# Output projection and router with fp32 operands in place of three fp16 products

## The chip, the cores and the metric

The kernel runs on one core of one Trainium2 chip. The metric is the device time of one launch in microseconds (us). Engines are named as in the profile: PE is TensorE (PEld its weight loads), DVE is VectorE, ACT is ScalarE, POOL is GpSimd, and SP issues most of the DMA transfers.

## What is computed

A block of a gated cross-attention model on 64 batches of 128 tokens with 256 features, all fp32: normalise, cross-attend to a context, add; normalise again, choose one of 32 experts by a router, run that expert's two-layer network, add.

```python
# x: (64, 128, 256), ctx: (64, 128, 192), 16 heads of 16, 32 experts of hidden size 64
x = x + tanh(g_xattn) * xattn(layernorm(x), ctx)
#   xattn: q = h @ wq + bq; k = y @ wk + bk; v = y @ wv + bv
#          out = softmax(q k^T / 4) v, heads side by side
#          return out @ wo + bo                      <- the output projection
x = x + tanh(g_ffn) * ffn(layernorm(x))
#   ffn: logits = h @ router_w.T + router_b          <- the router
#        e = argmax(logits)
#        return relu(relu(h @ w1[e] + b1[e]) @ w2[e] + b2[e])
```

## The kernel before

The program has two parts. The first goes over 16 groups of four batches (512 tokens). The second goes over 96 tiles of 128 tokens that a scatter has sorted by expert.

**The group loop.** Every engine runs the same software pipeline, and the engines are tied by semaphores only. In one step, `step(s)`, the group `s` is in its attention and output projection; `a` (two groups ahead) gets its normalised input transposed and its q, k and v; `n1` (one ahead) has its score maxima taken; `f` (one behind) is in its second normalisation and router; `r` (two behind) is ranked and scattered. The tensor engine's step has two phases. First come 16 chunks, each with scores (L1068), transposed scores (L1084) and the product with v (L1101, whose operands are fp32), between which ACT takes exponentials and DVE takes maxima. Then comes the tail, in this order: k and q of `a`, the transposes of the attention's output (L1199), v of `a`, the transposes of the normalised output (L1216), the transposes of the router's input (L1223), the output projection, and the router. q and k go through two DRAM images to be stacked by head (`q_image`, `k_image`, then `qstk`, `kstk`), and the next step's first scores wait for the last of these transfers. In the last two steps (groups 14 and 15) there is no group `a`, and so no k, q, v and no transfer of q in the tail.

**Three fp16 products.** q, k, the output projection, the router and the experts' products split each fp32 operand into a high fp16 part and a low fp16 rest, and multiply high by high, low by high and high by low into one PSUM bank. The pairs are in `THREE`, and all of these products are issued by `split_matmul` (L1148). For the output projection ACT copies the transposed output S[t] to fp16 (L721), DVE subtracts that copy from S[t] to get the low part (L846, called from L933), and PE waits for `at_lo` before its 24 products of 256 columns a group. For the router ACT copies AV[t] (L732), DVE subtracts (L846, from L936), and PE waits for `x2t_lo` before its 24 products of 32 columns. DVE then reads the projection (L945, `x2_done`) and the logits (L853, `lg_done`). The weights' two parts are made once, at the start (L638, L651 on ACT; L788, L800 on DVE).

`at` lies in the buffer `xt`, and `x2t` in the upper half of each row of `ot`. SP's queue is in order: after the stacks it issues the row of maxima (L418, waits for `m_done`) and the next residual input (L423, waits for `x2_done`).

Of the kernel before, what the change touches and what calls it, by code (L numbers as in the profile page):

```python
# [32 lines left out]
P = 128  # L33
# [7 lines left out]
KT = D // P  # L41
# [55 lines left out]
def build(nc, x, ctx_t, g2, wq, bq, wk, bk, wv, bv, wo, bo, rw, rb, w1, b1, w2, b2, out):  # L97
    es = ExitStack()
    with es:
# [26 lines left out]
        wq_s = sb("wq_s", [P, 2, KT, D], F16)  # L126
        wk_s = sb("wk_s", [P, 2, 2, D], F16)
        wv_s = sb("wv_s", [P, 2, 2, D], F16)
        wo_s = sb("wo_s", [P, 2, KT, D], F16)
        rw_s = sb("rw_s", [P, 2, KT, E], F16)  # L130
        rb_b = sb("rb_b", [P, E])
        bqk = sb("bqk", [P, 2, KT])
        bqk8 = sb("bqk8", [P, 2, KT])
# [35 lines left out]
        rec = sb("rec", [P, GB, HEADS])  # L169

        an = ot[:, :, 0:D]
        at = xt
        x2 = sb("x2", [P, 2, GB, ROW])
        st2 = sb("st2", [P, GB, 6])
        mv2 = sb("mv2", [P, GB, 2])
# [8 lines left out]
        bo_b = ot_flat[:, 2 * P:2 * P + D]  # L184
        b2raw = ot_flat[0:E, 4 * P:4 * P + D]
        rw_raw = ot_flat[:, 6 * P:6 * P + KT * E].rearrange("p (k e) -> p k e", k=KT)
        x2t = ot[:, :, D:2 * D].bitcast(F16)
        lg = sb("lg", [P, GB, E])
        lmax = sb("lmax", [P, GB])
        pick = sb("pick", [P, GB, E])  # L190
# [51 lines left out]
        ln1_st ln1_mv ln1_sm xn_done y_hi y_t xt_ready xt_hi xt_lo q_ready q_hi q_lo k_ready k_hi k_lo  # L242
        v_ready v_done
        s_ready s_max mt_ready m_done st_ready exp_done av_ready av_out o_ready nrm_r nrm_done at_ready
        at_hi at_lo xb_done y_ready x2_done ln2_st ln2_mv ln2_sm xn2_done x2t_ready x2t_hi x2t_lo
        lg_ready lg_done route hot_done rk_ready rk_read rk_link pos_done ids_done
        ew_r8 ew_hi ew_lo
        t_link p_rows t_cols t_tr t_rows
# [366 lines left out]
        def _(act):  # L615
# [16 lines left out]
            act.wait_ge(s_["bias_in"], 16 * 8)  # L632
            a_.activation(bqk8[:], bqk[:], ACT.Copy, scale=WS).then_inc(s_["w_hi"], 1)
            a_.activation(b2raw[:], b2raw[:], ACT.Copy, scale=WS).then_inc(s_["w_hi"], 1)
            a_.activation(rw_raw[:], rw_raw[:], ACT.Copy, scale=WS).then_inc(s_["w_hi"], 1)
            act.wait_ge(s_["w_hi"], 5)
            a_.copy(b2hl[:, 0, :], b2raw[:]).then_inc(s_["b2_hi"], 1)
            a_.copy(rw_s[:, 0, :, :], rw_raw[:]).then_inc(s_["b2_hi"], 1)  # L638
            a_.copy(bvb[:], bvc[:].unsqueeze(2).to_broadcast([P, KT, P])).then_inc(s_["bv_wide"], 1)
            act.wait_ge(s_["w_in2"], 32)  # L640
            scaled(wraw2[:, 0:2, :])
# [4 lines left out]
            act.wait_ge(s_["tanh_done"], 1)  # L646
            a_.activation(wraw2[:, 2:4, :], wraw2[:, 2:4, :], ACT.Copy, scale=WS).then_inc(s_["w_raw8"], 1)
            act.wait_ge(s_["w_raw8"], 7)
            a_.activation(wraw2[:, 2:4, :], wraw2[:, 2:4, :], ACT.Identity, scale=tg[:, 0:1]).then_inc(s_["w_raw8"], 1)
            act.wait_ge(s_["w_raw8"], 8)  # L650
            a_.copy(wo_s[:, 0, :, :], wraw2[:, 2:4, :]).then_inc(s_["w_hi"], 1)  # L651

            def exp_chunk(g, c):
                act.wait_ge(s_["st_ready"], g.count(CHUNKS, c + 1))
# [33 lines left out]
            def step(s):  # L688
                a, n1, g, f = s.plus(2), s.plus(1), s, s.plus(-1)
                for c in range(CHUNKS):  # L690
                    if g.real():
                        exp_chunk(g, c)
                        if c % 4 == 2 and c > 4:
                            attn_out(g, c // 4 - 1)
                    if n1.real() and c in MAX_ROW:
                        max_row(n1, MAX_ROW[c])
                if a.real():
                    for t in range(KT):
                        act.wait_ge(s_["xt_ready"], a.count(2, t + 1))
                        wait(act, s_["y_ready"], a.count(2, -4))  # L700
                        a_.copy(xt[:, 0, t, :], M[t][:]).then_inc(s_["xt_hi"], 1)
                if g.real():
                    attn_out(g, 3)
                for t in range(KT):
                    if a.real():
                        act.wait_ge(s_["k_ready"], a.count(2, t + 1))
                        wait(act, k_out, a.count(64))
                        a_.activation(ks[:, 0, t, :], ST[t][:], ACT.Identity, bias=bqk8[:, 1, t:t + 1]).then_inc(s_["k_hi"], 1)
                    if n1.real() and t == 0:
                        max_row(n1, 3)  # L710
                if a.real():
                    for t in range(KT):
                        act.wait_ge(s_["q_ready"], a.count(2, t + 1))
                        wait(act, q_out, a.count(64))
                        a_.activation(qs[:, 0, t, :], M[t][:], ACT.Identity, bias=bqk8[:, 0, t:t + 1]).then_inc(s_["q_hi"], 1)  # L715
                if g.real():
                    for t in range(KT):
                        act.wait_ge(s_["at_ready"], g.count(2, t + 1))
                        if a.real():
                            act.wait_ge(s_["q_ready"], a.count(2, 2))  # L720
                        a_.copy(at[:, 0, t, :], S[t][:]).then_inc(s_["at_hi"], 1)  # L721
                if a.real():
                    for t in range(2):
                        act.wait_ge(s_["v_ready"], a.count(2, t + 1))
                        wait(act, s_["av_ready"], a.count(CHUNKS, -CHUNKS))
                        vv = v[:, a.par, t * 1024:t * 1024 + 1024].rearrange("p (h d) -> p h d", d=32)[:, :, 0:DH]
                        a_.activation(vv, ST[t][:].rearrange("p (h d) -> p h d", d=DH), ACT.Copy,
                                      scale=1.0 / WS).then_inc(s_["v_done"], 1)
                if f.real():
                    for t in range(KT):  # L730
                        act.wait_ge(s_["x2t_ready"], f.count(2, t + 1))
                        a_.copy(x2t[:, t, :], AV[t][:]).then_inc(s_["x2t_hi"], 1)  # L732
                if a.real():

                    expert_raw(a)
                    expert_hi(a)
# [38 lines left out]
        def _(dve):  # L775
# [7 lines left out]
            dve.wait_ge(s_["w_hi"], 2)  # L783
            v_.tensor_tensor(wq_s[:, 1, :, :], wraw[:, 0:2, :], wq_s[:, 0, :, :], ALU.subtract).then_inc(s_["w_lo"], 1)
            v_.tensor_tensor(wk_s[:, 1, :, :], wraw[:, 2:4, :], wk_s[:, 0, :, :], ALU.subtract).then_inc(s_["w_lo"], 1)
            dve.wait_ge(s_["b2_hi"], 2)
            v_.tensor_tensor(b2hl[:, 1, :], b2raw[:], b2hl[:, 0, :], ALU.subtract).then_inc(s_["b2_lo"], 1)
            v_.tensor_tensor(rw_s[:, 1, :, :], rw_raw[:], rw_s[:, 0, :, :], ALU.subtract).then_inc(s_["w_lo"], 1)  # L788

            v_.memset(kstk[:, :, 0, :, :], 0.0).then_inc(s_["dve_set"], 1)  # L790
            dve.wait_ge(s_["w_hi"], 6)
# [4 lines left out]
            dve.wait_ge(s_["gb_a"], 1)  # L796
            dve.wait_ge(s_["tanh_done"], 1)
            v_.tensor_scalar(gbias[:], gbias[:], tg[:, 0:1], None, ALU.mult).then_inc(s_["gb_done"], 1)
            dve.wait_ge(s_["w_hi"], 7)
            v_.tensor_tensor(wo_s[:, 1, :, :], wraw2[:, 2:4, :], wo_s[:, 0, :, :], ALU.subtract).then_inc(s_["w_lo"], 1)  # L800
            dve.wait_ge(s_["pool_set"], 1)

            def x_stats(b):
# [78 lines left out]
            def step(s):  # L882
# [46 lines left out]
                if nxt.real():  # L929
                    stats_2(st1, mv1, "ln1_st", "ln1_mv", nxt, 0)  # L930
                if g.real():
                    for t in range(KT):
                        lo_part(at[:, 1, t, :], S[t][:], at[:, 0, t, :], "at_hi", g.count(2, t + 1), "at_lo")  # L933
                if f.real():
                    for t in range(KT):
                        lo_part(x2t[:, KT + t, :], AV[t][:], x2t[:, t, :], "x2t_hi", f.count(2, t + 1), "x2t_lo")  # L936
                if g.real():
                    dve.wait_ge(s_["xb_done"], g.count(1, 1))

                    pg = g.plus(-2)  # L940
                    if pg.real():
                        wait(dve, scat[pg.par], pg.halved(16 * GB, 16 * GB))
                    for t in range(2):
                        dve.wait_ge(s_["y_ready"], g.count(2, t + 1))
                        v_.scalar_tensor_tensor(out=x2[:, g.par, 2 * t:2 * t + 2, 0:D],  # L945
                                                in0=M[t][:].rearrange("p (b n) -> p b n", b=2), scalar=1.0 / WS,
                                                in1=xres[:, 2 * t:2 * t + 2, :], op0=ALU.mult, op1=ALU.add
                                                ).then_inc(s_["x2_done"], 1)
# [96 lines left out]
        def _(pe):  # L1045
# [5 lines left out]
                last = t_.matmul(AV[0][:, 0:D], bvb[:, t, :], wraw2[:, 2 + t, :], start=(t == 0), stop=(t == KT - 1))  # L1051
            last.then_inc(s_["bvwo_ready"], 1)
            pe.wait_ge(s_["pool_set"], 1)
            pe.wait_ge(s_["w_lo"], 5)

            def scores(n1, c):

                b, cc = c // 4, c % 4
                if c == 0:
                    pe.wait_ge(stk[n1.par], n1.halved(128, 128))  # L1060
                    wait(pe, s_["at_lo"], n1.count(2, -2))
                if c == 1:
                    wait(pe, s_["lg_done"], n1.count(1, -2))
                if c >= 2:
# [24 lines left out]
            def times_v(g, c):  # L1089
# [3 lines left out]
                if cc == 0:  # L1093
                    if b >= 2:
                        pe.wait_ge(s_["av_out"], g.count(4, b - 1))
                    else:
                        wait(pe, s_["x2t_lo"], g.count(2, -4 + b + 1))
                        wait(pe, s_["nrm_done"], g.count(4))
                for i in range(CH):
                    h = (b * HEADS + CH * cc + i) * 32  # L1100
# [52 lines left out]
            def step(s):  # L1153
# [70 lines left out]
                        last.then_inc(s_["x2t_ready"], 1)  # L1224
                if g.real():

                    pe.wait_ge(s_["at_lo"], g.count(2, 2))
                    if a.real():
                        pe.wait_ge(s_["q_lo"], a.count(2, 2))
                    elif n1.real():  # L1230
# [3 lines left out]
                    for b in range(GB):  # L1234
                        tok = slice(b * P, (b + 1) * P)
                        last = split_matmul(M[b // 2][:, (b % 2) * D:(b % 2) * D + D],
                                            [(at[:, i, t, tok], wo_s[:, j, t, :]) for t in range(KT) for i, j in THREE])
                        if b % 2:
                            last.then_inc(s_["y_ready"], 1)
                if f.real():  # L1240

                    pe.wait_ge(s_["x2t_lo"], f.count(2, 2))
                    for b in range(GB):
                        tok = slice(b * P, (b + 1) * P)
                        last = split_matmul(S[0][:, b * E:(b + 1) * E],
                                            [(x2t[:, i * KT + t, tok], rw_s[:, j, t, :]) for t in range(KT) for i, j in THREE])
                    last.then_inc(s_["lg_ready"], 1)

            schedule(pe, step)
# [95 lines left out]
```

## Time and profile before

| what | value |
|---|---|
| median of 3 runs | 1111.49 us (1101.32 to 1111.63) |
| span of the profiled execution | 1114.1 us |
| PE busy | 790.7 us (71%), 7430 instructions |
| PE weight loads busy | 531.1 us (48%) |
| DVE busy | 589.2 us (53%), 1575 instructions |
| ACT busy | 481.1 us (43%) |
| POOL busy | 481.3 us (43%) |
| mean granted clock of PE | 0.738 of full speed |

The profile is one execution; shares are of its span. Matmuls are pipelined, so a busy PE isn't PE at its peak. [...]

### The profile page before, as it was taken

To read this page: it belongs to the slowest core of one execution; us is meant where nothing else is said; L and a number is where in the kernel's file an instruction comes from. 1 tells how busy PE (TensorE), PEld (TensorE's weight loads), DVE (VectorE), ACT (ScalarE), POOL (GpSimd) and SP (SyncE) were. 2 spreads that over 40 slices of the span, in tenths; PEclk is the share of its full clock that TensorE was granted. 3 is DMA by queue.
4 is the path that set the end of the run, shared out by engine and by line. 5 is a ranking of instruction groups with operands and counts; after the bars stand their busy time and mean duration, and the time that the engine had idled before them with its cause. 6 is when DMAs were issued, how large, how long until landed. Compare 5 with 4: busy or idle time off the path is not lost.

```text
span 1114.1 us, 24048 instructions
## 1 busy us (share of the span) xinstructions
PE 790.7 (71%) x7430; PEld 531.1 (48%) x7431; DVE 589.2 (53%) x1575; ACT 481.1 (43%) x1045; POOL 481.3 (43%) x703
## 2 busy tenths in 40 slices
PE   0458696968677696969678686868775048878783
PEld 0235465645455465646445555646454035545451
DVE  3253455546455455545544565644534238677783
ACT  3223353435244343435343453524351037667673
POOL 9321324361626344352625344261333506555564
PEclk9765867669586867667695987958696558687886
DMA  3753627264553627173553527344210334343340
GB/s 90 175 106 85 114 64 156 63 125 87 100 112 95 115 74 160 49 143 79 108 106 100 115 85 154 82 67 102 53 31 29 134 94 131 107 126 109 109 114 19
DMA packets 76676, 110.55 MB, mean 99 GB/s; under 512 B 11542, under 2 KB 62875, under 8 KB 73504
## 3 DMA queue, kind: packets, MB, share of 16 engines
q1 hardware_dynamic: 68320, 90.61, 37.2%
q0 software_dynamic: 8256, 18.53, 4.7%
q8 instruction: 71, 1.16, 0.5%
q14 instruction: 29, 0.24, 0.1%
HBM read 70.68 MB, written 42.27 MB: 101 GB/s over the span
## 4 chain that ended last, share of the span: by engine, by line
PE 43%; DMA 21%; issue 15%; POOL 11%; DVE 3%; SPq 2%; ACT 2%; another core or an unknown queue 1%; POOLq 1%; ACTq 0%; DVEq 0%
DMA qstk<-q_image 14%; PE AV L1101 11%; PE S L1068 10%; PE ST L1084 8%; DMA q_image<-qs 7%; POOL out L604 6%; PE M L1148 4%; PE ST L1148 4%; PE M L1125 2%; POOL carry_p L471 1%; SPq L405 1%; POOL expert_rows L595 1%; DVE qs L848 1%; ACT qs L715 1%; PE M L1116 1%
## 5 line engine op out<-in xcount | busy, mean ns | idle before, releaser
L817 DVE TENSOR_REDUCE mx<-S 128x4 f32<-128x512 f32 x256 | 174.9, 689 | 304.0 <-PE S L1068 283.0
L657 ACT ACTIVATE pt<-ST 128x512 f32<-128x512 f32 x256 | 152.4, 596 | 349.9 <-PE ST L1084 336.8
L1068 PE MATMUL S<-kstk,qstk 96*128 96x128 f16 x1024 | 144.8, 290 | 155.6 <-DMA qstk<-q_image 141.6
L1068 PEld LDWEIGHTS S<-kstk,qstk 96*128 96x128 f16 x1024 | 90.5, 126 | 216.3 <-DMA qstk<-q_image 107.2
L1101 PE MATMUL AV<-pt,v 128*32 128x128 f32 x2048 | 147.0, 373 | 22.8 <-ACT pt L657 18.6
L528 POOL TENSOR_TENSOR w1s<-w1r,w1s 128x512 f32 (+1 forms) x16 | 18.4, 1150 | 328.5 <-ACT w2s L686 328.5
L1084 PE MATMUL ST<-qstk,kstk 98*128 98x128 f16 x1024 | 142.9, 285 | 0.1
L1084 PEld LDWEIGHTS ST<-qstk,kstk 98*128 98x128 f16 x1024 | 101.9, 134 | 4.4 <-issue 2.8
L1148 PE MATMUL ST<-qs,w1s 128*128 128x128 f16 x576 | 71.0, 259 | 20.9 <-ACT yin L755 9.9
L1101 PEld LDWEIGHTS AV<-pt,v 128*32 128x32 f32 x2048 | 48.0, 129 | 68.9 <-issue 37.7
L1267 PE MATMUL S<-ident,yin 128*128 128x128 f32 x192 | 47.8, 339 | 44.7 <-DVE yin L1012 32.1
L747 ACT CAST qs<-S 128x256 f16<-128x256 f32 x96 | 35.6, 371 | 91.6 <-PE S L1267 85.6
L587 POOL DMA_INDIRECT expert_rows<-x,posi x64 | 63.3, 990 | 17.2 <-issue 16.9
L1148 PEld LDWEIGHTS ST<-qs,w1s 128*128 x576 | 48.9, 112 | 45.0 <-issue 36.9
L471 POOL TENSOR_TENSOR carry_p<-zero_e 128x1 f32<-128x1 f32 x97 | 23.0, 237 | 105.3 <-DVE posn L1033 69.7
L1012 DVE TENSOR_SCALAR yin<-x 128x256 f32<-128x256 f32 x96 | 39.6, 412 | 33.8 <-DMA x<-expert_rows 33.2
L604 POOL DMA_INDIRECT out<-xin,posn x48 | 48.2, 1005 | 18.0 <-issue 18.0
L604 POOL DMA_INDIRECT out<-xn,posn x48 | 47.9, 999 | 17.9 <-issue 17.9
L1148 PE MATMUL M<-wo_s,xt 128*128 128x256 f16 x384 | 46.0, 278 | 11.2 <-DVE xt L846 11.2
L1267 PEld LDWEIGHTS S<-ident,yin 128*128 128x128 f32 x192 | 28.1, 173 | 53.4 <-DVE yin L1012 32.9
L565 POOL TENSOR_TENSOR ids<-ids,group_c 128x4 int32<-128x4 int32 x16 | 3.2, 198 | 113.0 <-DVE mv L810 113.0
L1018 DVE TENSOR_TENSOR qs<-S,qs 128x256 f16<-128x256 f32 x96 | 40.1, 418 | 15.5 <-ACT qs L747 15.1
(190 smaller groups left out, 1606.1 us busy)
## 6 DMA issues: line engine op xcount, KB each, us to landing
x<-expert_rows SPq DMA_DIRECT2D x96, 130.0 KB
xin<-x SPq DMA_DIRECT2D x16, 512.0 KB, 4.2
yin<-ctx_t SPq DMA_DIRECT2D x16, 512.0 KB, 5.2
k_image<-ks SPq DMA_DIRECT2D x64, 128.0 KB
q_image<-qs SPq DMA_DIRECT2D x64, 128.0 KB
kstk<-k_image SPq DMA_DIRECT2D x32, 256.0 KB, 6.7
qstk<-q_image SPq DMA_DIRECT2D x32, 256.0 KB, 8.9
xres<-x SPq DMA_DIRECT2D x16, 512.0 KB, 9.4
```

Source lines behind the costliest of these rows:

```text
L587: g_.indirect_dma_start(out=rows[:, :], out_offset=bass.IndirectOffsetOnAxis(ap=posi[:, b:b + 1], axis=0), in_=x2[:, r.par, b, :], in_offs ...
L604: g_.indirect_dma_start(out=out, out_offset=bass.IndirectOffsetOnAxis(ap=ido[:, m:m + 1], axis=0), in_=yo[m], in_offset=None, bounds_check ...
L657: a_.activation(pt[:, c % NPT, :], ST[c % 2][:], ACT.Exp, scale=0.25 / (WS * WS)).then_inc(s_["exp_done"], 1)
L747: a_.copy(gx[:, n % 2, 0, :, :], S[n % 2][:, 0:D].rearrange("p (k t) -> p k t", k=KT)).then_inc(s_["f_hi"], 1)
L817: v_.reduce_max(mx[:, b, CH * cc:CH * cc + CH], S[(c + 1) % 2][:].rearrange("p (h t) -> p h t", h=CH), X).then_inc(s_["s_max"], 1)
L1012: v_.tensor_scalar(gn[:, n % 2, :], gt[:, n, 0:D], gt[:, n, D:D + 1], gt[:, n, D + 1:D + 2], ALU.mult, ALU.add).then_inc(s_["f_norm"], 1)
L1018: v_.tensor_tensor(gx[:, n % 2, 1, :, :], S[n % 2][:, 0:D].rearrange("p (k t) -> p k t", k=KT), gx[:, n % 2, 0, :, :], ALU.subtract).then_ ...
L1068: last = t_.matmul(S[(c + 1) % 2][:, i * P:(i + 1) * P], qstk[0:STACK, n1.par, hp, b * P:(b + 1) * P], kstk[0:STACK, n1.par, cc // 2, hp, ...
L1084: last = t_.matmul(ST[c % 2][:, i * P:(i + 1) * P], kstk[0:STACK + 2, g.par, cc // 2, hp, b * P:(b + 1) * P], qstk[0:STACK + 2, g.par, hp, ...
L1101: last = t_.matmul(AV[b % 2][32 * i:32 * i + 32, cc * P:(cc + 1) * P], v[:, g.par, h:h + 32], pt[:, c % NPT, i * P:(i + 1) * P], start=Tru ...
L1148: last = t_.matmul(bank, w, m, start=(n == 0), stop=(n == len(pairs) - 1))
L1267: last = t_.transpose(S[n % 2][:, k * P:(k + 1) * P], gn[:, n % 2, k * P:(k + 1) * P], ident[:])
```

## The change

The weights `wo_s` and `rw_s` and the operands `at` and `x2t` are kept in fp32, in the same bytes as the two fp16 parts before. ACT's copies write fp32, DVE's four subtractions a group are gone with their semaphores, and each product is one `matmul` of fp32 operands, so eight a group in place of 24 for the projection and eight in place of 24 for the router. All waits on the low parts become waits on ACT's copies (`at_done`, `x2t_done`). The order of the work on each engine is otherwise the same.

```diff
-        wo_s = sb("wo_s", [P, 2, KT, D], F16)
-        rw_s = sb("rw_s", [P, 2, KT, E], F16)
+        wo_s = sb("wo_s", [P, KT, D])
+        rw_s = sb("rw_s", [P, KT, E])
-        at = xt
+        at = xt[:].rearrange("p a k t -> p (a k t)").bitcast(F32).rearrange("p (k t) -> p k t", k=KT)
-        x2t = ot[:, :, D:2 * D].bitcast(F16)
+        x2t = ot[:, :, D:2 * D]
...
-            a_.activation(wraw2[:, 2:4, :], wraw2[:, 2:4, :], ACT.Identity, scale=tg[:, 0:1]).then_inc(s_["w_raw8"], 1)
-            act.wait_ge(s_["w_raw8"], 8)
-            a_.copy(wo_s[:, 0, :, :], wraw2[:, 2:4, :]).then_inc(s_["w_hi"], 1)
+            a_.activation(wo_s[:], wraw2[:, 2:4, :], ACT.Identity, scale=tg[:, 0:1]).then_inc(s_["w_hi"], 1)
...
-                        a_.copy(at[:, 0, t, :], S[t][:]).then_inc(s_["at_hi"], 1)
+                        a_.copy(at[:, t, :], S[t][:]).then_inc(s_["at_done"], 1)
...
-                        a_.copy(x2t[:, t, :], AV[t][:]).then_inc(s_["x2t_hi"], 1)
+                        a_.copy(x2t[:, 2 * t:2 * t + 2, :], AV[t][:].rearrange("p (u n) -> p u n", u=2)).then_inc(s_["x2t_done"], 1)
...
-                    for t in range(KT):
-                        lo_part(at[:, 1, t, :], S[t][:], at[:, 0, t, :], "at_hi", g.count(2, t + 1), "at_lo")
-                if f.real():
-                    for t in range(KT):
-                        lo_part(x2t[:, KT + t, :], AV[t][:], x2t[:, t, :], "x2t_hi", f.count(2, t + 1), "x2t_lo")
-                if g.real():
...
-                    pe.wait_ge(s_["at_lo"], g.count(2, 2))
+                    pe.wait_ge(s_["at_done"], g.count(2, 2))
...
-                                            [(at[:, i, t, tok], wo_s[:, j, t, :]) for t in range(KT) for i, j in THREE])
+                                            [(at[:, t, tok], wo_s[:, t, :]) for t in range(KT)])
...
-                    pe.wait_ge(s_["x2t_lo"], f.count(2, 2))
+                    pe.wait_ge(s_["x2t_done"], f.count(2, 2))
...
-                                            [(x2t[:, i * KT + t, tok], rw_s[:, j, t, :]) for t in range(KT) for i, j in THREE])
+                                            [(x2t[:, 2 * t + b // 2, (b % 2) * P:(b % 2) * P + P], rw_s[:, t, :]) for t in range(KT)])
```

## Rows read from the trace of the kernel before

**Rows 1.** The page: chain of work that ended last, shares of the span by line.

```profile
DMA qstk<-q_image 14%; PE AV L1101 11%; PE S L1068 10%; PE ST L1084 8%; DMA q_image<-qs 7%; POOL out L604 6%; PE M L1148 4%; PE ST L1148 4%; PE M L1125 2%; POOL carry_p L471 1%; SPq L405 1%; POOL expert_rows L595 1%; DVE qs L848 1%; ACT qs L715 1%; PE M L1116 1%
```

**Rows 2.** The waits of all engines: who waited for whom; us in total, times, longest.

```profile
PE S L1068 <- DMA qstk<-q_image: 141.6, 15, 15.8
```

**Rows 3.** The chain that ended last, one step's tail: start, length, what.

```profile
518.72 2.60 PE M L1148 x12
523.28 4.83 DMA q_image<-qs
529.41 9.74 DMA qstk<-q_image
```

**Rows 4.** Timeline, same tail: start, length, engine, line [idle before it <- releaser].

```profile
525.72 1.07 ACT L721 CAST xt<-S 128x512 f16<-128x512 f32 x2 [3.68 <-PE S L1216]
525.95 1.04 PE L1223 MATMUL AV<-ident,xn 128*128 128x128 f32 x8
526.33 1.29 DVE L846 TENSOR_TENSOR xt<-S,xt 128x512 f16<-128x512 f32 x2 [1.37 <-ACT xt L721]
527.68 2.79 PE L1148 MATMUL M<-wo_s,xt 128*128 128x256 f16 x24 [0.69 <-DVE xt L846]
530.31 0.75 PE L1148 MATMUL S<-rw_s,ot 128*128 128x32 f16 x24
530.51 0.69 DVE L945 SCALAR_TENSOR_TENSOR x<-M,xres 128x512 f32<-128x512 f32 x1 [0.33 <-PE M L1148]
531.63 0.41 SPq L423 DMA_DIRECT2D xres<-x  x1
```

**Rows 5.** Groups by form, whole span: shapes xcount | busy us, mean ns | idle before.

```profile
L1051 PE MATMUL AV<-xres,ot 128*128 128x256 f32 x4 | 2.1, 671 | 12.9 <-ACT ot L639 12.9
L1051 PEld LDWEIGHTS AV<-xres,ot 128*128 128x128 f32 x4 | 1.2, 323 | 12.7 <-ACT ot L639 12.6
L664 ACT COPY ot<-AV 128x512 f32<-128x512 f32 x64 | 37.2, 581 | 2.6 <-PE AV L1101 2.6
```

**Rows 6.** Timeline at the start of the span, PE and PEld.

```profile
12.89 2.07 PE L1051 MATMUL AV<-xres,ot 128*128 128x256 f32 x4 [12.89 <-ACT ot L639]
28.29 1.94 PE L1125 MATMUL M<-ident,xn 128*128 128x128 f32 x8 [13.33 <-POOL xn L558]
30.45 0.15 PEld L1148 LDWEIGHTS ST<-ys,wk_s 128*128 128x128 f16 x1 [0.28 <-issue]
```

**Rows 7.** Window: stretch, length, PE, PEld, DVE, ACT, POOL busy, granted clock, DMA, GB/s.

```profile
12.90:15.00 2.10, 2.06 (x4) 1.16 (x4) 1.30 (x3) 1.18 (x4) 2.04 (x5) 1.00 0.00 0
```

**Rows 8.** The chain after the last transfer of q: start, length, what.

```profile
816.39 1.30 DVE xt L846 x2
...
821.12 0.25 PE ST L1084 x4
...
844.95 3.86 PE M L1148 x24
...
849.52 0.20 DVE lg L853
...
859.68 0.70 DVE ot L846
860.43 1.65 PE S L1148 x24
```

**Rows 9.** Windows of one wait, two chunk loops and group 15's projection.

```profile
629.00:631.00 2.00, 1.78 (x35) 1.57 (x33) 1.67 (x4) 1.43 (x3) 0.22 (x1) 1.00 1.02 176
635.00:637.00 2.00, 0.00 (x0) 0.00 (x0) 0.00 (x0) 0.00 (x0) 1.78 (x3) 0.67 1.08 142
637.90:662.50 24.60, 21.28 (x276) 14.15 (x277) 15.25 (x37) 11.89 (x24) 14.60 (x26) 0.77 0.25 87
733.90:762.20 28.30, 27.76 (x276) 17.97 (x277) 15.40 (x37) 12.17 (x24) 12.66 (x21) 0.50 0.12 41
844.00:849.00 5.00, 5.00 (x44) 4.02 (x43) 2.83 (x5) 1.17 (x2) 0.00 (x0) 0.67 0.00 0
```

More of the change, by code:

```diff
@@ L244, in build @@
         s_ready s_max mt_ready m_done st_ready exp_done av_ready av_out o_ready nrm_r nrm_done at_ready
-        at_hi at_lo xb_done y_ready x2_done ln2_st ln2_mv ln2_sm xn2_done x2t_ready x2t_hi x2t_lo
+        at_done xb_done y_ready x2_done ln2_st ln2_mv ln2_sm xn2_done x2t_ready x2t_done
         lg_ready lg_done route hot_done rk_ready rk_read rk_link pos_done ids_done
@@ L634, in _ @@
             a_.activation(b2raw[:], b2raw[:], ACT.Copy, scale=WS).then_inc(s_["w_hi"], 1)
-            a_.activation(rw_raw[:], rw_raw[:], ACT.Copy, scale=WS).then_inc(s_["w_hi"], 1)
+            a_.activation(rw_s[:], rw_raw[:], ACT.Copy, scale=WS).then_inc(s_["w_hi"], 1)
             act.wait_ge(s_["w_hi"], 5)
             a_.copy(b2hl[:, 0, :], b2raw[:]).then_inc(s_["b2_hi"], 1)
-            a_.copy(rw_s[:, 0, :, :], rw_raw[:]).then_inc(s_["b2_hi"], 1)
             a_.copy(bvb[:], bvc[:].unsqueeze(2).to_broadcast([P, KT, P])).then_inc(s_["bv_wide"], 1)
@@ L785, in _ @@
             v_.tensor_tensor(wk_s[:, 1, :, :], wraw[:, 2:4, :], wk_s[:, 0, :, :], ALU.subtract).then_inc(s_["w_lo"], 1)
-            dve.wait_ge(s_["b2_hi"], 2)
+            dve.wait_ge(s_["b2_hi"], 1)
             v_.tensor_tensor(b2hl[:, 1, :], b2raw[:], b2hl[:, 0, :], ALU.subtract).then_inc(s_["b2_lo"], 1)
-            v_.tensor_tensor(rw_s[:, 1, :, :], rw_raw[:], rw_s[:, 0, :, :], ALU.subtract).then_inc(s_["w_lo"], 1)
             v_.memset(kstk[:, :, 0, :, :], 0.0).then_inc(s_["dve_set"], 1)
@@ L798, in _ @@
             v_.tensor_scalar(gbias[:], gbias[:], tg[:, 0:1], None, ALU.mult).then_inc(s_["gb_done"], 1)
-            dve.wait_ge(s_["w_hi"], 7)
-            v_.tensor_tensor(wo_s[:, 1, :, :], wraw2[:, 2:4, :], wo_s[:, 0, :, :], ALU.subtract).then_inc(s_["w_lo"], 1)
             dve.wait_ge(s_["pool_set"], 1)
@@ L1053, in _ @@
             pe.wait_ge(s_["pool_set"], 1)
-            pe.wait_ge(s_["w_lo"], 5)
+            pe.wait_ge(s_["w_lo"], 3)
+            pe.wait_ge(s_["w_hi"], 7)
             def scores(n1, c):
@@ L1060, in scores @@
                     pe.wait_ge(stk[n1.par], n1.halved(128, 128))
-                    wait(pe, s_["at_lo"], n1.count(2, -2))
+                    wait(pe, s_["at_done"], n1.count(2, -2))
                 if c == 1:
@@ L1096, in times_v @@
                     else:
-                        wait(pe, s_["x2t_lo"], g.count(2, -4 + b + 1))
+                        wait(pe, s_["x2t_done"], g.count(2, -4 + b + 1))
                         wait(pe, s_["nrm_done"], g.count(4))
```

## Prediction

> **What bounds the kernel now.** I read the chain of work that ended last first [rows 1]. Its largest line isn't an engine's but a transfer: q going out to its image and coming back stacked has 7% and 14% of the span. The waits say the same from the other side [rows 2]: PE stood 141.6 us, 15 times, before a step's first scores until the last stack had landed, 9.4 us a time. Then I followed one step's tail in the chain [rows 3]. q's products end at 521.3, the image is written from 523.28 to 528.1, the stack lands at 539.15, and the scores start at once. Neither the output projection nor the router is in this piece of the chain. The timeline [rows 4] shows where they are: the projection runs from 527.68 to 530.47, the router to 531.06, and PE then waits 8.1 us for the transfer. So in every step that still has a group `a`, that is in 14 of the 16 steps with an output projection, the whole change lies under a DMA. It is on the path only after the last transfer of q, and there the chain names its lines three times [rows 8]: the projection of group 14 with the router behind it, the projection of group 15, and the last router.
>
> **What is removed.** DVE loses four subtractions a group, 64 in all, of 0.65 us each (two in 1.29) [rows 4], about 42 us. In the covered tails this is worth nothing to the end: it lets PE start the projection earlier (ACT's copies end at 526.79, PE's transposes at 526.99, against 527.68), in a stretch that ends in an 8.1 us wait. If that cover were gone it would be worth 0.7 us a step. At the start of the span the weights' low parts go too (under 1 us of DVE); PE's next work there waits for POOL until 28.29 [rows 6], so I take nothing.
>
> **What is swapped on ACT.** The copies keep their shape and write fp32. A copy to fp32 of this shape took 581 ns on average [rows 5], two casts to fp16 1.07 us [rows 4]. I take no change.
>
> **What is added on PE, the projection.** In place of 24 fp16 products of 256 columns there are eight fp32 ones. The trace of before has two fp32 products of just this shape, L1051, and they are four records [rows 5]: an fp32 product is two records, so a group has 16. The four took 2.07 us [rows 6], with the 0.67 us that the last one lasts [rows 5]: (2.07 - 0.67) / 3 = 0.47 us a record. Which clock was that? The window prints 1.00 there [rows 7], but eight fp32 transposes of 128 columns soon after took 1.94 us [rows 6], and in the tail, at 1.00, eight take 1.04 us [rows 4]. [...] From the other side: 24 fp16 products took 2.79 us, some 0.2 of it the last one's end, 0.108 us each; an fp32 record at twice that is 0.216. I take 0.213, so 16 x 0.213 = 3.4 us and the same end, 3.6 us, against 2.79 us: +0.85 us a group at the full clock.
>
> **The router.** Its 16 records have 32 columns only, so here the weight load sets the pace. fp16 needs 0.75 us for 24, 31 ns each [rows 4]. An fp32 load of 128 columns took 323 ns at the lower clock [rows 5] and an fp16 one 150 ns [rows 6]; the surplus of 173 ns is 86 ns at the full clock. So 31 + 86 = 117 ns a record, 1.9 us for 16: +1.1 us a group. The bounds: below, fp32 loads go as fast as fp16 ones, 16 x 31 ns = 0.5 us; above, a record here takes as long as one of the 256-column records, 16 x 0.22 = 3.5 us at the full clock and 7 us at the lower. I take 1.9 us, which is nearer to a row of the same instruction. The same two ends hold for the projection: its loads hidden (3.6 us) or in series, 16 x (0.213 + 0.117) = 5.3 us.
>
> [...]
>
> **The covered tails after it.** Projection from 526.99 to 530.6, router to 532.4, and then 6.7 us of waiting in place of 8.1. Even with loads in series (5.3 us) and the router at its upper end (3.5 us), PE ends at 535.8, 3.4 us before the transfer. DVE's second read of the projection moves from 530.51 to about 530.7, so SP's residual load (531.63 [rows 4], into the stack's transfer) moves by a few tenths at most. What is queued behind it on SP is the next inputs, 10 us later. I take 0 for all 14.
>
> **The exposed ones** [rows 8]. Group 14: DVE's two subtractions kept PE from 816.9 to 817.74; that is -0.85. Then +0.85 for the projection and +1.1 for the router, behind which the next group's transposed scores (821.12) are queued on PE. Sum +1.1. Group 15: here PE was busy with transposes until 844.95 and waited for nobody, so nothing is saved. The projection took 3.86 us, at a mean granted clock of 0.67 [rows 9]; times 16 x 2 / 24 it is 5.15, +1.3. Its router ended unseen, under DVE's read of the projection; now 1.9 us of it stand between 850.1 and the logits, which ran at 849.52: 852.0, so +2.5 for the group. Last router: -0.70 for the subtraction; 1.65 us for 24 at the lower clock become 16 x 0.234 + 0.1 = 3.85, +2.2; sum +1.5. All behind it, the ranks, scatters and expert tiles, moves along unchanged. Together 1.1 + 2.5 + 1.5 = **+5.1 us**. With all lower bounds the three are -0.3, +1.3 and -1.1, about 0; with all upper ones about +3, +5 and +5, and 4 more for loads in series, some +16.
>
> The sum is made against the profiled execution: 1114.1 + 5.1 = 1119.2 us of span. The median shown is 1111.49, 2.6 below that span, so 1116.6 us.
>
> **Forecast and rivals.**
>
> *The forecast, chance 0.52:* hidden in 14 steps, +5.1 us in the last ones, clocks on average as before. Own range 1111 to 1122.
>
> *The clock rises later in some chunk loops, 0.15.* After every wait for the stack PE starts at 0.50. In one loop it rose about 11 us in and the loop took 24.6 us; in another it stayed down to the end, 28.3 us [rows 9]. Of the 13 loops whose windows I read, six were of the first kind and seven of the second, and I see no regular pattern. Each step's start moves by nothing, but PE's tail is of another make, and if two or three loops more fall into the second kind, each costs 3.7 us: +7 to +11, so 1124 to 1128. This is the case on the slow side; it decides from two loops on. For it: the three runs of before differ by 10 us, as much as three loops. Against it: nothing in the change acts during the loop.
>
> *The same to the other side, 0.12:* two or three loops more rise early, 1105 to 1109.
>
> *The shorter wait keeps the clock up, 0.08.* The clock fell 2 to 5 us after PE's last work; latest in the step whose PE work ended at 630.8, where it fell at 635.7 and the scores began at 637.9 [rows 9] (a window's mean gives the moment). If PE ends 1.4 us later, or 4 us later with loads in series, a wait can end before the fall. The loop would then run at 1.00 from its start. From a mean of 0.50 to one of 0.77 it gained 3.7 us [rows 9], so from there to 1.00 about 3.2 us more, 3.2 to 6.9 us a step. Three or four such steps give -10 to -28, from 1116.6 to between 1089 and 1107. Against it: 6.7 us less the spread of the waits stays above 4.9. [...]
>
> *fp32 loads aren't hidden, 0.08:* projection 5.3 us, so +2 in group 14, +2.5 in group 15, still covered elsewhere: 1119 to 1124.
>
> *Something not in these, 0.05*, such as the engines' instruction fetches falling elsewhere: either side.
>
> **How the numbers follow.** Forecast 1116.6 us. Leaving out a tenth at each end takes the range from 1105 (into the early-clock case) to 1126 (into the late one). About 1% is what a measurement of this kernel can tell from no change, so 1100.4 and 1122.6 are the marks. Slower by over 1%: the late-clock case (0.13 of its 0.15), a third of the loads in series (0.03), a little of the forecast and half of the rest: 0.19. Faster: the kept clock (0.06), a little of the early one and the rest: 0.10. Within: 0.71.
>
> **What would show it.** Right: 256 records each for projection and router; a covered projection of about 3.6 us that starts right at the end of L1223; a router of about 1.9 us; a first-scores wait for the stack near 8 us on average in place of 9.4; 64 fewer L846 instructions; the stretch from the end of the last stack to the end of the last router (862.1) longer by 5 us. Wrong: a projection record of 0.43 us at the full clock (then the tail fills the cover and PE becomes its bound); windows at 1.00 right before the first scores; or a transfer of the stack that takes another time than 9 to 10 us.

## The result and the profile after

The changed kernel took 1116.95 us (median of 20 runs, 1107.08 to 1130.13) against 1108.81 us (20 runs, 1093.54 to 1120.97): a ratio of 1.011, 95% interval 1.008 to 1.014. The forecast was 1116.6 us. Ratios are taken over the runs within 1.5% of the fastest; since both kernels' times spread evenly over some 2.5%, I give the medians of all runs as well: +8.1 us here, and +8.6 us when the changed kernel was run again on another chip. So the sign was right, and the change is some 8 us rather than the 5.1 us of the sum. How well is that known? The ratio's interval means +9 to +16 us, and if the two sets of 20 times are drawn again at random, the difference of their medians lies between +3 and +17 us in 95 of 100 draws. That the forecast time came within 0.4 us of the measured one is luck: the three runs on which it stood had a median 2.7 us above that of the 20, and the change costs about 3 us more than the sum said.

One covered tail, from the timeline of the changed kernel (start, length, engine, line), to be read against [rows 4]; L1212 is the former L1223, L1137 the former L1148, L1057 the former L1068:

```profile
523.44 1.04 PE L1212 MATMUL AV<-ident,xn 128*128 128x128 f32 x8
524.33 3.72 PE L1137 MATMUL M<-wo_s,xt 128*128 128x256 f32 x16
527.89 1.87 PE L1137 MATMUL S<-rw_s,ot 128*128 128x32 f32 x16
537.17 0.61 PE L1057 MATMUL S<-kstk,qstk 96*128 96x128 f16 x4 [7.42 <-DMA qstk<-q_image]
```

The projection follows the transposes at once, takes 3.7 us and the router 1.9 us with their ends, and 7.4 us of waiting are left. Over the span the wait is 8.3 us a time, against 9.4 [rows 2]; here 16 waits are counted, there 15, and over the same 15 it is 7.9 against 9.1:

```profile
PE S L1057 <- DMA qstk<-q_image: 133.0, 16, 16.5
```

The shares of the chain that ended last, against [rows 1]:

```profile
DMA qstk<-q_image 13%; PE AV L1090 12%; PE S L1057 10%; PE ST L1073 9%; DMA q_image<-qs 7%; POOL out L604 6%; PE M L1137 4%; PE ST L1137 4%; PE M L1114 2%; POOL carry_p L471 1%; ACT pt L654 1%; SPq L405 1%; POOL expert_rows L595 1%; DVE qs L842 1%; ACT qs L712 1%
```

The groups by form, to be read against the fp32 records of [rows 5]:

```profile
L1137 PE MATMUL M<-wo_s,xt 128*128 128x256 f32 x256 | 59.3, 385 | 0.7 <-ACT xt L718 0.7
L1137 PE MATMUL S<-rw_s,ot 128*128 128x32 f32 x256 | 31.6, 279 | 0.7 <-ACT ot L729 0.7
```

The chain after the last transfer of q, to be read against [rows 8]:

```profile
817.93 3.45 PE M L1137 x16
821.38 1.70 PE S L1137 x16
...
843.16 1.94 PE S L1188 x8
...
852.05 3.46 PE M L1137 x16
855.51 1.72 PE S L1137 x16
...
867.53 3.64 PE S L1137 x16
```

Up to the first scores after the last transfer of q the profiled executions are alike: 784.5 us before, 783.3 after. From there to the end of the last router it is 77.6 us before and 87.9 after; from there to the end of the span 252.0 and 252.5. So all of the difference between these two executions, 10 us, lies in the exposed stretch, and it splits up:

| piece | before | after | difference |
|---|---|---|---|
| chunk loop of group 14 | 25.4 | 25.7 | +0.3 |
| group 14's tail (first transposes to router's end) | 11.2 | 14.1 | +2.9 |
| chunk loop of group 15 (router's end to next transposes) | 15.4 | 20.1 | +4.7 |
| group 15's tail | 12.9 | 14.1 | +1.2 |
| from there to the last router's end | 12.7 | 14.0 | +1.3 |

The third row is a piece in which nothing was changed. The windows say why. Before (stretch, length, PE, PEld, DVE, ACT, POOL busy, granted clock, DMA, GB/s), behind group 13's router that ends at 821.1:

```profile
821.00:823.00 2.00, 1.54 (x33) 0.94 (x29) 2.00 (x9) 1.25 (x3) 0.00 (x0) 1.00 0.19 34
823.00:834.00 11.00, 9.74 (x172) 5.23 (x164) 2.64 (x15) 9.33 (x17) 8.97 (x15) 1.00 0.16 55
```

After, behind the same router that ends at 823.1:

```profile
823.00:825.00 2.00, 1.54 (x29) 0.94 (x27) 1.88 (x8) 1.25 (x3) 0.00 (x0) 0.89 0.73 244
825.00:836.00 11.00, 11.00 (x126) 5.46 (x119) 4.89 (x14) 6.76 (x12) 8.26 (x15) 0.50 0.02 6
```

PE's granted clock, given as a share of its full speed, fell to 0.50 at about 824.6, 1.5 us behind the fp32 router, in which PE had been idle for half a microsecond. It had been idle as long before the change (1.54 us busy of 2.00 in both). In the next 11 us PE issued 126 records where it had issued 172.

### The profile page after: what moved, and what is told of

Same layout as the page of the kernel before. It is cut to its first block, busy times and chain, and to the rows that moved or that the text cites. A ratio compares the mean times of both kernels' runs of the same rounds, so it can differ in the third digit from the quotient of the medians.

```text
span 1123.7 us, 23464 instructions
## 1 busy us (share of the span) xinstructions
PE 833.4 (74%) x7174; PEld 565.3 (50%) x7175; DVE 551.5 (49%) x1509; ACT 480.6 (43%) x1043; POOL 481.5 (43%) x703
## 4 chain that ended last, share of the span: by engine, by line
PE 44%; DMA 21%; issue 14%; POOL 11%; SPq 3%; DVE 2%; ACT 2%; another core or an unknown queue 1%; POOLq 1%; ACTq 0%; DVEq 0%
DMA qstk<-q_image 13%; PE AV L1090 12%; PE S L1057 10%; PE ST L1073 9%; DMA q_image<-qs 7%; POOL out L604 6%; PE M L1137 4%; PE ST L1137 4%; PE M L1114 2%; POOL carry_p L471 1%; ACT pt L654 1%; SPq L405 1%; POOL expert_rows L595 1%; DVE qs L842 1%; ACT qs L712 1%
## 5 line engine op out<-in xcount | busy, mean ns | idle before, releaser
L1057 PE MATMUL S<-kstk,qstk 96*128 96x128 f16 x1024 | 144.4, 289 | 135.0 <-DMA qstk<-q_image 133.0
L1057 PEld LDWEIGHTS S<-kstk,qstk 96*128 96x128 f16 x1024 | 90.4, 126 | 196.6 <-DMA qstk<-q_image 98.3
L1090 PE MATMUL AV<-pt,v 128*32 128x128 f32 x2048 | 151.8, 384 | 22.1 <-ACT pt L654 17.9
L528 POOL TENSOR_TENSOR w1s<-w1r,w1s 128x512 f32 (+1 forms) x16 | 18.4, 1153 | 329.6 <-ACT w2s L683 329.6
L1073 PE MATMUL ST<-qstk,kstk 98*128 98x128 f16 x1024 | 146.1, 290 | 0.3 <-issue 0.2
L1137 PE MATMUL ST<-qs,w1s 128*128 128x128 f16 x576 | 70.5, 255 | 21.2 <-ACT yin L752 9.6
L1137 PEld LDWEIGHTS ST<-qs,w1s 128*128 x576 | 47.6, 110 | 46.4 <-issue 38.4
L933 DVE SCALAR_TENSOR_TENSOR x<-M,xres 128x512 f32<-128x512 f32 x32 | 22.1, 692 | 82.5 <-PE M L1137 82.5
L1137 PE MATMUL M<-wo_s,xt 128*128 128x256 f32 x256 | 59.3, 385 | 0.7 <-ACT xt L718 0.7
L1000 DVE TENSOR_SCALAR yin<-x 128x256 f32<-128x256 f32 x96 | 40.3, 420 | 34.8 <-DMA x<-expert_rows 34.1
```

The lines of the kernel that those rows point to most:

```text
L1000: v_.tensor_scalar(gn[:, n % 2, :], gt[:, n, 0:D], gt[:, n, D:D + 1], gt[:, n, D + 1:D + 2], ALU.mult, ALU.add).then_inc(s_["f_norm"], 1)
L1057: last = t_.matmul(S[(c + 1) % 2][:, i * P:(i + 1) * P], qstk[0:STACK, n1.par, hp, b * P:(b + 1) * P], kstk[0:STACK, n1.par, cc // 2, hp, ...
L1073: last = t_.matmul(ST[c % 2][:, i * P:(i + 1) * P], kstk[0:STACK + 2, g.par, cc // 2, hp, b * P:(b + 1) * P], qstk[0:STACK + 2, g.par, hp, ...
L1090: last = t_.matmul(AV[b % 2][32 * i:32 * i + 32, cc * P:(cc + 1) * P], v[:, g.par, h:h + 32], pt[:, c % NPT, i * P:(i + 1) * P], start=Tru ...
L1137: last = t_.matmul(bank, w, m, start=(n == 0), stop=(n == len(pairs) - 1))
```

## The experiments

Two questions: is the cost only in the exposed stretch (theory A) or also in the 14 covered tails (theory B), and is the fall of the clock behind group 13's router made by the fp32 router or chance? The times:

| kernel | median, us (runs) | before on the same chip (runs) | difference of medians | ratio, 95% interval |
|---|---|---|---|---|
| projection only | 1112.99 (12) | 1112.53 (35) | +0.5 | 0.995, 0.990 to 1.000 |
| router only | 1118.18 (12) | 1112.53 (35) | +5.7 | 1.004, 0.999 to 1.009 |
| covered steps only | 1109.07 (12) | 1112.53 (35) | -3.5 | 0.997, 0.993 to 1.000 |
| exposed steps only | 1118.37 (12) | 1112.53 (35) | +5.8 | 1.005, 1.000 to 1.009 |
| the change again | 1114.47 (12) | 1105.90 (29) | +8.6 | 0.999, 0.995 to 1.004 |
| the change, group 13's router fp16 | 1112.51 (12) | 1105.90 (29) | +6.6 | 1.005, 1.001 to 1.008 |
| before, 24 products in the wait | 1106.61 (12) | 1105.90 (29) | +0.7 | 0.985, 0.979 to 0.992 |
| before, 34 products in the wait | 1071.63 (6) | 1105.90 (29) | -34.3 | 0.964, 0.958 to 0.969 |
| the same again | 1088.05 (6) | 1114.77 (11) | -26.7 | 0.970, 0.963 to 0.977 |
| before, 34 narrow fp32 products | 1148.84 (6) | 1114.77 (11) | +34.1 | 1.034, 1.029 to 1.039 |
| the change, 28 products in the wait | 1099.02 (6) | 1114.77 (11) | -15.8 | 0.985, 0.978 to 0.992 |
| before, 40 products in the wait | 1087.90 (6) | 1114.77 (11) | -26.9 | 0.975, 0.968 to 0.981 |

The times of one kernel spread over some 25 us, so these differences are known to 5 us or so, not better. Drawing the runs again at random gives, in 95 of 100 draws, -11 to +6 us for the projection only, -4 to +10 for the router only, -7 to +1 for the covered steps only, +1 to +10 for the exposed ones, -2 to +13 for the change again and +1 to +10 with group 13's router in fp16. For the change again the two measures differ: +8.6 us by the medians, no difference by the ratio (0.999), which hangs on one run of 1099 us. So that run bears out the sign and not the size.

**One operand pair alone.** Projection only (`proj32` is true for every group and `rout32` for none; the line with `THREE` stays behind the `else`):

```diff
+                                            [(at32[:, t, tok], wo_f[:, t, :]) for t in range(KT)] if proj32(g) else
```

> Only the output projection is fp32; the router keeps its three fp16 products. Theory A (the cost lies after the last transfer of q, and the fp32 router makes the clock fall in group 14's tail): the last chunk loop stays at the clock of 1.00 as before (about 14.4 us from the router's end to the next transposes), and the kernel is 0 to 2 us slower than before. Theory B (the cost lies in the 14 covered tails): the larger part of the PE time added there is the projection's (0.7 us against the router's 0.9), so about 5 us slower.

Router only (the other way round):

```diff
+                                            [(x2t32[:, 2 * t + b // 2, (b % 2) * P:(b % 2) * P + P], rw_f[:, t, :]) for t in range(KT)]
+                                            if rout32(f) else
```

> Only the router is fp32; the projection keeps its three fp16 products. Theory A: +1 us in group 14, +1.3 in group 15, +1.5 in the last router, and the last chunk loop at the lower clock for +4: 7 to 9 us slower than before. Theory B: about 6 us slower, and nothing particular after the last transfer of q.

The projection alone costs nothing that can be told (+0.5 us, expected 0 to 2 by theory A and 5 by B); the router alone costs +5.7 us, less than the 7 to 9 of theory A and near the 6 of B. That points to A, but given the uncertainty above these two times alone don't decide. The profiles say more. The last chunk loop kept 1.00 with the fp16 router (16.2 us) and lost it right behind the fp32 router (20.0 us), which ends at 816.5 (windows of the router-only kernel):

```profile
816.00:818.00 2.00, 1.54 (x25) 1.16 (x24) 1.45 (x6) 1.09 (x2) 0.00 (x0) 1.00 0.47 138
818.00:829.00 11.00, 11.00 (x128) 5.50 (x125) 4.95 (x16) 6.55 (x12) 8.08 (x15) 0.50 0.08 26
```

**Covered steps alone, exposed steps alone.** Each kernel chooses the form by the step; the weights of the other form are made on DVE in the wait at step 14. Shown is the kernel with the covered steps; the one with the exposed steps has `n >= 14` and `n >= 13`.

```diff
+def proj32(g):
+    n = g.off if isinstance(g.base, int) else 2
+    return n < 14
...
+def rout32(g):
+    n = g.off if isinstance(g.base, int) else 2
+    return n < 13
```

> Both are fp32 in the 14 steps whose tail lies under the transfer of q, and three fp16 products in the last three steps (groups 14 and 15 of the projection, 13 to 15 of the router). Its fp16 parts are made on DVE in a stretch in which DVE waits. Theory A: same time as before, within 3 us, and the stretch after the last transfer of q as long as before (77.6 us from the first scores to the last router's end). Theory B: the whole cost, 8 to 12 us.

> The counterpart: fp32 only in the last three steps, three fp16 products in the 14 covered ones. Theory A: the whole cost, 8 to 12 us, with a stretch from the first scores after the last transfer of q to the last router's end of 86 to 88 us in place of 77.6, and the last chunk loop at the clock of 0.50. Theory B: 1 to 2 us.

The covered steps cost nothing (-3.5 us, its interval reaching from a gain of 0.7% to none), the exposed ones cost +5.8 us. Theory B, which wanted 8 to 12 and 1 to 2 us, falls with the first of the two; theory A's 8 to 12 us for the exposed steps was too much. The start of the first scores after the last transfer of q says the same of the covered part: 783.3, 776.0, 781.4 and 783.4 us in the profiles whose covered tails are all fp32 (the change twice, group 13's router in fp16, covered only), 784.5 and 775.2 us in those whose covered tails are all fp16 (before, exposed only). But in the profile of the exposed-only kernel the clock did not fall behind group 13's router, which ends at 813.2:

```profile
813.00:815.00 2.00, 1.54 (x30) 1.00 (x29) 1.78 (x8) 1.20 (x3) 0.00 (x0) 1.00 0.70 216
815.00:826.00 11.00, 9.79 (x172) 5.23 (x164) 2.71 (x15) 9.29 (x17) 8.98 (x15) 1.00 0.06 22
```

so here the expectation of 0.50 missed, and its stretch from those first scores to the last router's end is 79.6 us, not 86 to 88. Covered only missed as well, with 81.2 us where 77.6 was expected, though nothing in the stretch is changed there. Over the profiles the stretch splits by the clock and not by the edit: 77.6 to 81.5 us where the last chunk loop kept 1.00 (before, projection only, covered only, exposed only, group 13's router in fp16), 85.1 to 88.4 us where it lost it (router only, the change twice). The fall behind the fp32 router is therefore likely, not certain.

**The change again, and with one router of 16 undone.** The second keeps all of the change but group 13's router (`rout32` returns `n != 13`).

> The changed kernel itself, on the chip of the next three. Theory A (cost only after the last transfer of q): +5 us for the exposed projection and routers, and in profiles where the clock falls right behind group 13's fp32 router some 4 to 5 us more; +5 to +10 in all. The covered part (start to the first scores after the last transfer) within the scatter of before. Theory B (a further cost in the covered tails): more than 10.

> The changed kernel with one of its 16 routers, that of group 13 in group 14's tail, done in three fp16 products again (its fp16 weights are made on DVE in a wait). Theory A with the clock: the last chunk loop keeps 1.00 (15.4 to 16.2 us in place of 20.1), the router is 1.1 us shorter: 3 to 6 us faster than the changed kernel. Rival (the clock's fall there was chance): 1 us faster, and the clock falls behind it as often as not.

The change again gave +8.6 us by the medians, inside theory A's 5 to 10 (the ratio shows none of it), and its profile has the fall once more (clock 0.91 in the 2 us behind the router, then 0.50; loop 20.3 us). With the one router undone the loop has 1.00 and 15.4 us, as expected (its router ends at 817.9):

```profile
817.00:819.00 2.00, 1.54 (x40) 1.25 (x40) 1.62 (x5) 0.79 (x2) 0.00 (x0) 1.00 0.02 4
819.00:830.00 11.00, 10.55 (x184) 5.63 (x178) 3.44 (x18) 9.19 (x17) 8.41 (x15) 1.00 0.17 56
```

But its median is only 2.0 us below the change's, short of the 3 to 6 expected and within the scatter of the two: by time alone this run is inconclusive. The verdict comes from the profiles together. Behind an fp32 router of group 13 the clock fell in four of five, each time 1.4 to 1.5 us after the router's end: the change twice, router only and the change with 28 products below, with loops of 20.1, 20.3, 20.0 and 19.3 us; not in exposed only, 15.5 us. Behind an fp16 one it fell within 10 us in none of nine: before, projection only, covered only, this one and the five profiles below of kernels that are built on the one before. One rival is that the clock had risen only just before and would have dropped anyway. The same profiles speak against it: at the end of the fp16 router the clock had been up for 3.0 to 8.1 us, at the end of the fp32 one for 5.4 us (the change, the change with 28 products) and 8.7 us (router only, the change again) where it fell, and 9.2 us where it did not.

**What the clock is worth, and what holds it.** The kernel before, with products in the wait that nobody reads:

```diff
                     last.then_inc(s_["lg_ready"], 1)
+                if a.real():
+                    pe.wait_ge(s_["v_done"], a.count(2, 2))
+                    for _ in range(34):
+                        t_.matmul(ST[1][:], wq_s[:, 0, 0, 0:P], wk_s[:, 0, :, :], start=True, stop=True)
```

> The kernel before, and at the end of each step that waits for the transfer of q PE runs 24 fp16 products of 512 columns into a free PSUM bank, 5.2 us of work that nobody reads. It tests the rival of the kept clock and the price of the clock's fall. If PE's clock bounds the chunk loop: the wait left is about 3 us, the clock falls 1.8 to 4.9 us after PE's last work, so half of the loops start at 1.00 and gain 3 to 7 us each: 20 to 45 us faster. Rival (the loop is bound by DVE and ACT): no difference.

> The same with 34 products, 7.3 us; the wait left is about 1 us, and none where a transfer is quick. If PE's clock bounds the chunk loop: nearly all loops start at 1.00, 40 to 80 us faster. Rival: no difference, or some us slower where the products outlast a transfer.

> The kernel before with 34 fp16 products of 512 columns in each wait, once more, beside the next three. 30 to 40 us faster than before if the first measurement holds.

> The kernel before with 40 products, 8.6 us, in each wait. Where the transfer is quick they outlast it by up to 1.5 us; where it is slow they save a fall of the clock. Within 5 us of the one with 34, and with less spread, if the clock is what counts.

34 products bring 27 to 34 us, less than the 40 to 80 expected of the first run and the 30 to 40 of the second: the price of a kept clock was right, the number of steps that keep it was not. In the five profiles with wide products in the wait, the stretch from a step's first scores to the transposes in its tail took 21.0 to 27.6 us, 26.0 on average, where the clock held through the wait and deep into the loop, and 31.0 on average where it fell in the wait or soon behind it. But of 15 waits it held in 2 with 24 products, in 5 and 7 with 34, in 10 with 40, and in 5 in the changed kernel with 28; in another nine of the first run with 34, PE did start at 1.00, as expected, and lost it within 2.6 us. The timeline of the second run's profile shows PE's row at one wait, and the window behind it:

```profile
526.19 7.50 PE L1251 MATMUL ST<-wk_s,wq_s 128*128 128x512 f16 x34
534.67 0.40 PE L1068 MATMUL S<-kstk,qstk 96*128 96x128 f16 x4 [0.98 <-DMA qstk<-q_image]
```

```profile
537.00:545.00 8.00, 7.86 (x142) 5.31 (x141) 7.62 (x24) 5.30 (x10) 4.20 (x12) 1.00 0.53 182
```

The idle time is 1 us, the loop starts at 1.00, and four scores take 0.40 us instead of 0.61. At the next wait the transfer landed 3.6 us after the last of the 34, the clock fell just as PE went on, and the window behind has 0.50 again:

```profile
583.00:589.00 6.00, 5.92 (x61) 4.11 (x62) 4.76 (x12) 2.39 (x4) 0.39 (x1) 0.50 0.69 237
```

With 24 products the wait left is about 3 us; the times spread from 1081 to 1118 us with a median like before's, so the expected 20 to 45 us did not come: too few waits were short enough. 40 products are as good as 34 beside them, within the 5 us expected. They hold the clock more often, but they take 8.8 us where 34 take 7.5 and can outlast the transfer. The spread was narrower with 40, as expected (18.7 us against 26.0), though with six runs each that is weak.

The narrow ones are the router's own form, 32 columns of fp32 (against the kernel with 34 wide ones):

```diff
+                    pe.wait_ge(s_["gb_done"], 1)
+                    pe.wait_ge(s_["bias_in"], 128)
...
-                        t_.matmul(ST[1][:], wq_s[:, 0, 0, 0:P], wk_s[:, 0, :, :], start=True, stop=True)
+                        t_.matmul(ST[1][:, 0:E], gbias[:, 0:P], rb_b[:], start=True, stop=True)
```

> The same, but each of the 34 is an fp32 product with 32 columns, the router's own form: two records of 0.107 us, so PE is occupied for the same 7.3 us. Theory (narrow fp32 products do not hold the clock, which is why it falls right behind group 13's fp32 router): the clock falls inside or right behind these products, the chunk loops start at 0.50, and the gain of 34 us is gone or nearly. Rival (PE being occupied is enough): as fast as with the wide products.

They are 34 us slower than before, 61 us slower than the same number of wide ones. PE's row and the windows of one wait:

```profile
550.07 9.75 PE L1253 MATMUL ST<-rb_b,gbias 128*128 128x32 f32 x68
```

```profile
552.00:554.00 2.00, 2.00 (x21) 2.00 (x20) 0.00 (x0) 0.00 (x0) 2.00 (x3) 1.00 0.94 98
554.00:556.00 2.00, 2.00 (x18) 2.00 (x18) 0.00 (x0) 0.00 (x0) 1.78 (x3) 0.88 0.87 135
556.00:558.00 2.00, 2.00 (x11) 2.00 (x11) 0.00 (x0) 0.00 (x0) 1.76 (x3) 0.50 1.08 132
562.00:570.00 8.00, 8.00 (x85) 5.00 (x81) 5.93 (x19) 2.93 (x6) 2.50 (x8) 0.50 0.55 182
```

PE and its weight load are busy for all of every window, and the clock falls to 0.50 at about 555.5, 5.4 us after the narrow products began. From there a record takes nearly twice as long (start to start 213 ns instead of 112), so 68 records took 9.7 us here. At the next wait the fall came 2.5 us after the first of them and they took 12.4 us:

```profile
603.00:605.00 2.00, 2.00 (x13) 2.00 (x12) 0.00 (x0) 0.00 (x0) 2.00 (x3) 0.57 0.82 152
```

So it goes at every wait: the clock fell inside the narrow products in all 16, 2.5 to 5.7 us after their start, and inside the wide ones, which last 5.3 to 8.8 us, in none of the 80 waits of the five profiles that have them. "Occupied is enough" falls; that narrow fp32 products don't hold the clock stands, and it is the likely cause of the fall behind group 13's router, which is of the same form but lasts only 1.7 us.

The 34 us over the kernel before are not slower loops in the main, since its loops begin at 0.50 too. From the end of q's products to the next scores a step takes 20.2 us on average instead of 18.4, because the narrow products outlast the transfer; the rest of the step takes 31.9 instead of 31.3. Over 14 steps the first makes 26 us and the second 7.

The change with the same products in the wait, 28 of them because its tail is longer:

```diff
+                    for _ in range(28):
+                        t_.matmul(ST[1][:], wq_s[:, 0, 0, 0:P], wk_s[:, 0, :, :], start=True, stop=True)
```

> The changed kernel with 28 fp16 products of 512 columns in each wait: its tail is 1.65 us longer, so 28 end about where 34 do in the kernel before. Most loops start at 1.00 as there; +5 us for the exposed part and up to 4 for the last chunk loop: 5 to 10 us slower than the kernel before with 34, some 25 us faster than before.

1099.0 us, 11 us behind the kernel before with 34 (1088.1), a little over the 5 to 10 expected, and 15.8 us faster than before, where some 25 were expected. With six runs each these are known to 10 us or so. So the version that beats both kernels is the one before with 34 or 40 wide products in each wait, 2.5 to 3.6% faster than before.

## Why the prediction was right, and where its sum was short

**The cover.** Right. The projection starts with the end of the transposes instead of 0.7 us later, PE ends later all the same, and the wait behind it is 8.3 us on average, where about 8 were foretold; the covered-only kernel was not slower (-3.5 us, at most +1).

**The price of the projection.** Right: 3.45 us in the chain against 3.4 to 3.6. In the changed kernel the records of the projection start 0.216 us apart at a granted clock of 1.00, where the sum had 0.213; in the kernel before, the fp16 records of the same 256 columns start 0.109 us apart. That L1051's 0.47 us a record belonged to the lower clock was my estimate from the durations of the transposes: no window shows it, since the one there prints 1.00. In the trace the last three of the four records start 0.427 us apart, twice what the projection's do. At that pitch 16 records would have been 6.9 us.

**The price of the router.** 1.70 to 1.72 us in the chain against 1.9. From start to start its records are 112 ns apart at 1.00, where the sum had 117. At the lower clock (0.50) the last router took 3.64 us against 3.85, with records 213 ns apart where the sum had 234. The term of 86 ns for the slower load took L1051's 323 ns for a load at the lower clock, which no window shows either. What the traces show in its place is the step between the two forms at 1.00: fp16 records of the router start 25 ns apart in the kernel before, fp32 ones 112 ns in the changed one, 87 ns more. The weight load was busy all the time in both: 0.60 of 0.60 us in the window 530.35:530.95 before, 1.70 of 1.70 us in 527.90:529.60 after.

**Group 14.** +1.1 foretold. Router-only and exposed-only have 12.4 us where before has 11.2: +1.2. In the changed kernel's own profile it is +2.9, because its chunk loop had ended at 0.50 and eight transposes before the projection took 1.97 us where before had 1.09. That 1.7 us is most likely the clock's scatter: the change again has 12.5 us for this tail, and kernels with an fp16 router there have up to 12.4 us (13.2 in projection only, whose projection began at the lower clock).

**Group 15.** +2.5 foretold, +1.2 measured. The projection was scaled from 3.86 us at a mean clock of 0.67 [rows 9]; in the changed kernel it ran at 1.00 and took 3.46. The logits behind it waited for the router as foretold. That the clock is up here is again scatter, not something the sum had foreseen.

**Last router.** +1.5 foretold, +1.3 measured.

**What was missing.** The clock behind group 13's router. The terms above, as measured, make +1.2 + 1.2 + 1.3 = +3.7 us (5.1 foretold). The chunk loop of group 15 adds +4.7 us where the clock falls; in four of five profiles it did, so some 3.8 us on average, and the two make 7.5 us against 8.1 and 8.6 of the medians. Since the medians are known to 5 us or so, this agreement proves little, and the run with the one router undone did not show the 4 us in its time. In the sum the loop between the two tails stood at nothing. I had the late-rising clock as a rival of chance, with "nothing in the change acts during the loop" against it. That sentence was the step that failed: the router's new form acts, as far as the profiles show, on the clock just ahead of the loop.

**The rival of the kept clock.** It did not come, but "stays above 4.9" was a little off: the shortest wait of the changed kernel was 4.6 us, and the clock fell 3.7 us into it. I priced the wait by its length alone, while what PE did ahead of it matters too. After the end of PE's work the clock fell within 1.6 us in 18 of 60 waits in the four profiles whose covered tails have both products in fp32 (0.8 us at the soonest), and in none of 60 in before, projection only, exposed only (1.8 us at the soonest) and router only (1.7 us). So an fp32 router alone did not bring this about; it took the fp32 projection ahead of it too.

**The range and the number.** The range was wide enough for all of this mainly because the clock's scatter had been put into it. The number itself was hit by two errors that cancel: +2.7 us in the median of before and -3.0 us in the sum. One of the lower bounds was also added up wrongly: a last router of 0.5 us gives 0.5 - 1.65 - 0.70 = -1.85 us and not -1.1. Nothing hangs on it.

## What to carry to other kernels

Ask first whether the edited work lies under a transfer: 14 of 16 places here cost nothing that could be measured, in either direction, and the time was decided in the two places behind the last transfer. Measure each shape by itself: in the covered tail shown above, 8 fp32 products in place of 24 fp16 ones took 3.72 us instead of 2.79 at 256 columns, a third more, and 1.87 us instead of 0.75 at 32, two and a half times as much. Look also at what fills a wait of PE. Here it waited 9.4 us a time before the change and 8.3 after it, and started at 0.50 behind every one of the waits; 34 or 40 wide products held the clock in 5 to 10 of 15 waits and brought 27 to 34 us, three to four times what the change cost. And when the times of one kernel spread over 25 us, an effect of 4 us has to be read from profiles; a dozen runs don't show it.

## What the runs showed of the hardware that I had not expected

The 128 fp32 products of the projection left 256 records in the changed kernel, and so did the router's 128, two a product. From start to start a record took 0.216 us for 256 columns and 0.112 us for 32 at a granted clock of 1.00, and 0.213 us for 32 at 0.50. PE fully occupied by such products of 32 columns still lost the clock in 16 of 16 waits, after 5.4 us at one (0.88, then 0.50, at a busy share of 1.0) and 2.5 us at the next; and behind the router of 1.7 us it was lost within 1.5 us in four of five profiles. Whether their narrowness or their type does it was not told apart: no run had narrow fp16 products of that length.
